# VectorE transposes the two 2-byte halves itself, with a lagging chain and moved issues, in a four-layer graph network on one core

## The chip, the cores and the metric

One core of a Trainium2 chip runs the kernel; the other cores are idle. The metric is the device time of one execution in microseconds. TensorE (PE) has a matrix queue and a weight-load queue (PEld), VectorE is DVE, ScalarE is ACT, GpSimd is POOL, and SyncE (SP) only issues transfers here. ACT issues transfers too.

## The reference

`x` is 2048 x 64, `adj` is 2048 x 2048 and holds zeros and ones. Four layers follow one another, each `x = layernorm(x + layer(x))`:

```python
# layer 0
deg = jnp.clip(jnp.sum(adj, axis=1, keepdims=True) + 1.0, 1.0, None)
h_neigh = (adj @ X + X) / deg
out = relu(concatenate([X, h_neigh], axis=1) @ W + b)
out / maximum(norm(out), 1e-12)
# layer 1
h = tanh(concatenate([X, tcol], axis=1) @ W1 + b1)
h @ W2 + b2 + adj @ (X @ B.T) - sum(adj, axis=1) * (X @ B.T)
# layer 2: the last up to 100 neighbours of a row, each weighted half as much as the next
rank = cumsum(adj != 0, axis=1); deg = rank[:, -1:]; k = minimum(deg, 100)
w = mask * where(rank - (deg - k) > 0, 0.5 ** (deg - rank), 0)
w @ (x @ weight) + bias
# layer 3
x_proj = tanh(|x|) * x / |x|
out = arctanh(|y|) * y / |y|, y = adj @ x_proj
out @ kernel + bias
```

## The kernel before

The nodes are cut into 16 blocks of 128 rows (NB), and the rows of `adj` into 4 chunks e of 512 (NE, CW). The transposed matrix stays in SBUF as `AT` (bf16), and the decayed weights of layer 2 as `WT` (int16, the exponent of a bf16).

**Loading.** Block m of `adj` (1 MB) goes to one of 8 slots (4 in `stage`, 4 in `WT`). Its lower half is two transfers issued by SP (`load_lower`), its upper half two issued by ACT (`load_upper`). Blocks 8 to 15 wait until the block in their slot is transposed. SP also issues the packed weights (417 KB), between blocks 0 and 1. In `pack(m)` (L247) POOL copies the upper two bytes of one set of words beside those of the other set, and `transposes(m)` (L464) moves the 1,024 pairs of a partition as 4-byte words through DVE's 32 x 32 transpose. `counts(e)` of PE waits for blocks 4e to 4e+3.

**Layer 0, the chain and a part of layer 1.** For each chunk e PE runs `counts(e)`, the 16 matmuls of `sums(0, e)` (`sum_block`, L687) with `degrees(e)` in their middle, `add_own`, and then `chain(n)` for n = 16e to 16e+15. A step of the chain is two matmuls of 512 columns (L752, L754) into one of two banks of `psC`; `take_chain(n)` of ACT (L361) evicts the bank, and step n+2 waits for it. `dense(0, e)` stands behind the second step. In chunk 3, 12 of the steps carry two matmuls each of layer 1.

ACT has, in order, 16 issues of blocks 0 to 7 ahead of its first eviction, and then in each chunk `take_counts`, `take_sum`, further issues (blocks 8 to 11 behind the sum of chunk 0, 12 and 13 behind that of chunk 1, 14 and 15 in the chain of chunk 1), and the 16 evictions.

DVE has in each chunk four `transposes`, `take_degrees`, `activate0` (which waits for POOL's `weigh` and for `dense(0, e)`), `combine0`, and `normalise` of the chunk before. `normalise` ends in `split`, which writes `XP`, the input of the next layer. POOL has the roots (`l2_root`, `var_root`, powers with a fixed time), `residual`, and `diagonals` (four instructions a chunk).

**Layers 1 to 3.** The rest of layer 1 (`transpose_x`, `hidden`, sums, `dense(1, e)`) stands behind the whole chain. Layers 2 and 3 have 64 sum matmuls each. PE runs groups 0, 1 and 2 (blocks 4g to 4g+3) over all four chunks, then the last group chunk by chunk with `dense(l, e)` behind it. Between the two layers DVE runs `add_residual`, `variance` and `exp_map(e)` for each chunk; `exp_map(e)` ends in `split`, and group g of layer 3 waits for `split` of chunk g. `take_sum(2, 3)` stands on ACT behind `norm_tanh(0)` and `squares(2, 2)`. Behind layer 3 come `norm_in`, `log_map` and `normalise(3, e)` on DVE, and 16 transfers of the output, issued by SP as the chunks of X come.

## Time and profile before

| | us |
|---|---|
| median of 3 runs | 185.96 (184.53 to 732.64) |
| profiled execution | 186.58 |
| its span | 184.6 |
| PE busy | 133.7 |
| DVE busy | 93.2 |
| ACT busy | 65.9 |
| POOL busy | 70.3 |

The span runs from the first to the last instruction; 1.98 us of the profiled execution lie around it. Rows of a timeline give the start, the duration, the engine, the line and the tiles, and in brackets the idle time before. Durations of neighbouring matmuls overlap, so their pitch is read from starts. `x8` is eight instructions merged into a row; a matmul with float32 operands runs as two.

### The profile page before, as it was taken

The page shows a single profiled execution, that of the slowest core. Times are in us where ns is not written, and L with a number is a line of the kernel's source. Part 1 is how long each engine was busy: PE and PEld are TensorE (multiplying, and loading weights), DVE is VectorE, ACT ScalarE, POOL GpSimd, SP SyncE. Part 2 cuts the span into 40 slices and gives each one's busy share as a digit, 9 for nine tenths or more (in the row PEclk, how much of TensorE's full clock was granted, in tenths as well). Part 3 has the DMA queues.
Part 4 walks back from the last instruction along what each step waited for, and adds up shares of the span by engine and source line. Part 5 has one row for each costly group of instructions (what it writes and reads, how often), then busy time and mean ns, then how long its engine had stood idle before and what let it go on. Part 6 is the DMA issues. An engine that isn't in the chain of part 4 may idle for free.

```text
span 184.6 us, 2088 instructions
## 1 busy us (share of the span) xinstructions
PE 133.7 (72%) x728; PEld 68.6 (37%) x728; DVE 93.2 (50%) x224; ACT 65.9 (36%) x122; POOL 70.3 (38%) x78
## 2 busy tenths in 40 slices
PE   0010799959998699889998999999992799970000
PEld 0000793511243135124543447874452544660000
DVE  0752773309948967951562000176326766068940
ACT  0001511138827664782767344400041300372100
POOL 0021535054596589374181000255308444032440
PEclk9999999978999999999999999999998599998555
DMA  6999999999999980000000000000000000000022
GB/s 140 264 260 326 340 340 325 209 208 276 269 286 221 249 172 12 0 0 0 4 0 0 0 0 4 0 0 0 4 0 0 0 0 2 0 0 0 0 56 57
DMA packets 13929, 18.58 MB, mean 101 GB/s; under 512 B 5472, under 2 KB 5600, under 8 KB 13920
## 3 DMA queue, kind: packets, MB, share of 16 engines
q1 hardware_dynamic: 8256, 9.81, 21.2%
q10 hardware_dynamic: 5664, 8.65, 18.1%
q8 instruction: 5, 0.08, 0.2%
q14 instruction: 4, 0.03, 0.1%
HBM read 17.93 MB, written 0.52 MB: 100 GB/s over the span
## 4 chain that ended last, share of the span: by engine, by line
PE 62%; ACTq 12%; ACT 9%; DVE 8%; issue 3%; POOL 2%; POOLq 1%; DVEq 0%
PE psS L687 20%; ACTq L328 12%; PE psC L687 10%; ACT WT L361 7%; PE psC L752 7%; PE psC L754 5%; PE psN L722 4%; PE psH L731 3%; PE psN L787 2%; PE psN L786 2%; PE psH L760 2%; POOL root L264 1%; PE psX L711 1%; PE psH L789 1%; PE psC L749 1%
## 5 line engine op out<-in xcount | busy, mean ns | idle before, releaser
L361 ACT ACTIVATE WT<-psC 128x512 int16<-128x512 f32 x64 | 36.2, 596 | 14.7 <-PE psC L754 9.4
L264 POOL TENSOR_TENSOR root<-var,power 128x4 f32<-128x4 f32 (+1 forms) x16 | 18.7, 1173 | 44.5 <-DVE var L516 27.5
L687 PE MATMUL psS<-AT,XP 128*128 128x512 bf16 x128 | 34.2, 403 | 0.0
L752 PE MATMUL psC<-AT,cb 128*128 128x512 bf16 x56 | 22.5, 403 | 6.7 <-ACT WT L361 6.0
L754 PE MATMUL psC<-AT,cb 128*128 128x512 bf16 x64 | 25.1, 393 | 0.0
L687 PEld LDWEIGHTS psS<-AT,XP 128*128 128x128 f16 x128 | 12.6, 104 | 17.1 <-issue 5.5
L247 POOL COPY stage<-stage 128x1024 bf16<-128x1024 bf16 x10 | 13.3, 1327 | 12.2 <-DMA stage<-adj 12.2
L711 PE MATMUL psX<-cb,XP 128*128 128x128 bf16 x32 | 4.0, 264 | 19.1 <-DVE XP L598 12.9
L464 DVE STREAM_TRANSPOSE AT<-stage 128x1024 f32<-128x1024 f32 x10 | 12.4, 1242 | 8.6 <-POOL stage L247 8.6
L687 PE MATMUL psC<-AT,XP 128*128 128x512 bf16 x64 | 15.4, 379 | 0.6 <-ACT WT L361 0.6
L752 PEld LDWEIGHTS psC<-AT,cb 128*128 128x128 bf16 x56 | 5.5, 99 | 26.4 <-ACT WT L361 24.8
L532 DVE TENSOR_TENSOR t<-psN,XB 128x256 f32<-128x256 f32 x6 | 2.5, 420 | 25.3 <-PE psN L787 19.7
L372 ACT ACTIVATE v<-t 128x256 f32<-128x256 f32 x12 | 5.0, 416 | 20.8 <-DVE t L532 16.0
L277 POOL TENSOR_TENSOR XB<-X,weights 128x256 f32<-128x256 f32 x12 | 9.2, 770 | 5.9 <-DVE X L521 5.9
L270 POOL TENSOR_SCALAR diag<-cb,ndeg 128x128 f16<-128x128 bf16 x16 | 11.0, 703 | 0.0
L464 DVE STREAM_TRANSPOSE AT<-WT 128x1024 f32<-128x1024 f32 x6 | 7.4, 1240 | 7.0 <-POOL WT L247 6.9
L521 DVE TENSOR_TENSOR X<-t,root 128x256 f32<-128x256 f32 x16 | 6.8, 423 | 8.3 <-POOL root L264 8.2
L711 PEld LDWEIGHTS psX<-cb,XP 128*128 128x128 f16 x32 | 3.0, 126 | 20.7 <-issue 14.0
L247 POOL COPY WT<-WT 128x1024 bf16<-128x1024 bf16 x6 | 8.0, 1346 | 5.0 <-DMA WT<-adj 5.0
L687 PEld LDWEIGHTS psC<-AT,XP 128*128 128x128 f16 x64 | 6.1, 99 | 7.2 <-issue 1.3
L355 ACT ACTIVATE stage<-psS 128x512 f32<-128x512 f32 x6 | 3.6, 597 | 13.9 <-PE psS L687 13.3
L283 POOL TENSOR_TENSOR nroot<-n,power 128x8 f32<-128x8 f32 x2 | 3.3, 1642 | 12.8 <-DVE n L552 12.8
(124 smaller groups left out, 214.2 us busy)
## 6 DMA issues: line engine op xcount, KB each, us to landing
stage<-adj ACTq DMA_DIRECT2D x20, 256.0 KB, 11.4
stage<-adj SPq DMA_DIRECT2D x20, 256.0 KB, 14.5
WT<-adj ACTq DMA_DIRECT2D x12, 256.0 KB, 16.2
WT<-adj SPq DMA_DIRECT2D x12, 256.0 KB, 17.9
out<-X SPq DMA_DIRECT2D x16, 32.0 KB, 1.6
weights<-weights_packed SPq DMA_DIRECT2D x1, 417.5 KB, 12.1
X<-x SPq DMA_DIRECT2D x2, 128.0 KB, 2.9
X<-x ACTq DMA_DIRECT2D x2, 128.0 KB, 3.6
```

The costliest lines, as they stand in the source:

```text
L247: nc.gpsimd.tensor_copy(halves[:, :, 1, :, 0], halves[:, :, 0, :, 1]).then_inc(packed, 1)
L264: nc.gpsimd.tensor_tensor(root[:, e, 0:n], var[:, e, 0:n], power[:, 0:n, 0:NR], ALU.pow).then_inc(root_ready, 1)
L270: last = nc.gpsimd.tensor_scalar(diag[:, c], C("paired"), ndeg[:, c:c + 1], None, ALU.mult)
L277: nc.gpsimd.tensor_tensor(XB[:, chunk(e)], X[:, chunk(e)], per_feature(W(f"b{l}")), ALU.add).then_inc(xb_ready, 1)
L328: act.dma_start(slot(slot_of(m))[QD * q:QD * (q + 1)], ad[m, q]).then_inc(filled[slot_of(m)], 16)
L361: nc.scalar.activation(WT[:, e, chain_block(bank, k)], psC[bank][:], ACT.Relu).then_inc(chain_taken, 1)
L464: nc.vector.transpose(words.rearrange("p c (k b) -> p k c b", k=2), src.rearrange("p k (c a) -> p k c a", a=QD)).then_inc(transposed, 1)
L687: ins = nc.tensor.matmul(bank, XP[:, l % 2, c], matrix, start=(c == 0), stop=last)
L711: ins = nc.tensor.matmul(psX[:, P * r:P * (r + 1)], XP[:, l % 2, NR * e + r], C("ident"), start=True, stop=True)
L722: ins = nc.tensor.matmul(psN[e % 2][:, D * r:D * (r + 1)], xt0[:, e % 2, P * r:P * (r + 1)], W("WA"), start=True, stop=True)
L752: nc.tensor.matmul(acc, C("past"), AT[:, c + 1, e], start=False, stop=False, skip_group_check=True)
L754: nc.tensor.matmul(acc, C("own"), AT[:, c, e], start=False, stop=True, skip_group_check=(k > 0)).then_inc(chain_ready, 1)
```

## The change

- `pack` is gone. `transposes(m)` waits for the transfers themselves and is two instructions. Each takes the upper two bytes of 1,024 words of a partition, read two bytes out of every four, and writes them two bytes out of every four.
- The weights go in two transfers: 128 columns (with `WA`, `b0`) behind block 0, the other 707 columns behind block 3. ACT issues blocks 4 to 7 one by one behind the four `take_xt(0, e)`, blocks 8 to 11 behind the first four evictions, 12 to 15 in the chain of chunk 1.
- The chain lags: steps 11 to 15, and 27 to 31, run inside the sums of the next chunk. Steps 42 to 55 follow the sums of chunk 3 with one matmul of layer 1 each in 12 of them. Ahead of chunk 3 PE runs parts of layer 1 (`transpose_x(1, 0)` and `(1, 1)`, `hidden(0)` and `(1)`, 12 sum matmuls), and steps 56 to 63 carry 12 sum matmuls of chunk 2 behind `dense(1, 0)`. The banks are dealt out anew for this.
- Layer 2 begins inside layer 1, and runs groups 2 and 3 together, chunk by chunk. ACT takes the sums 2 and 3 of layer 2 earlier. `exp_map` uses `t` times the root in place of X, and `normalise(2, e)` moves behind its `split`.
- In the tail ACT multiplies by the gain (`project`, 4 instructions of 128x64 a chunk) and rescales chunks 0 and 1 (`rescale`, 4 a chunk). `log_map` is cut in two. `diagonals` is one instruction a chunk.

```diff
-WCOLS = {"WA": 64, "WB": 64, "W1": 128, **{name: 64 for name in CENTRED}, "I": 64,
-         "b0": 64, "w1t": 1, "h_bias": 1, "t": 1}
+WCOLS = {"WA": 64, "b0": 64, "WB": 64, "W1": 128, **{name: 64 for name in CENTRED}, "I": 64,
+         "w1t": 1, "h_bias": 1, "t": 1}
...
         def sum_bank(l, e):
-            return psS[e % 2] if l == 0 else (psS + psC)[e]
+            return psS[0] if l == 0 else (psS[1], psN[1], psS[0], psC[0])[e]
...
-            return psN[e % 2] if l < 2 else (psN + [psX, psH])[e]
+            return psN[0] if l == 0 else (psN[0], psH)[e % 2] if l == 1 else (psN[0], psH, psX, psC[1])[e]
+
+        CHAIN_IN_SUMS = (0, 11, 27, 42)
+        CHAIN_LOOP = 56
+        CHAIN_ALL = NB * NE
...
             load_lower(0)
-            sp.dma_start(weights[:], wpack).then_inc(weights_loaded, 16)
-            for m in range(1, NB):
+            sp.dma_start(weights[:, 0:first], wpack[:, 0:first]).then_inc(own_weights_loaded, 16)
+            for m in range(1, NR):
+                load_lower(m)
+            sp.dma_start(weights[:, first:WTOT], wpack[:, first:WTOT]).then_inc(weights_loaded, 16)
+            for m in range(NR, NB):
                 load_lower(m)
...
-            def pack(m):
-                pool.wait_ge(filled[slot_of(m)], 16 * NQ * (fills_before(m) + 1))
-                halves = slot(slot_of(m)).rearrange("p Q j -> p (Q j)").bitcast(BF16).rearrange(
-                    "p (k h j w) -> p k h j w", k=2, h=2, w=2)
-                nc.gpsimd.tensor_copy(halves[:, :, 1, :, 0], halves[:, :, 0, :, 1]).then_inc(packed, 1)
...
+            def project(e):
+                act.wait_ge(gain_ready, e // 2 + 1)
+                rows = dense_bank(3, e)[:].rearrange("p (r f) -> p r f", r=NR)[:, :, 0:D]
+                for r in range(NR):
+                    c = NR * e + r
+                    ins = nc.scalar.activation(t[:, c], rows[:, r], ACT.Copy, scale=gain[:, c:c + 1])
+                ins.then_inc(projected, 1)
+
+            def rescale(e):
+                act.wait_ge(root_ready, layer_chunk(3, e) + 1)
+                for r in range(NR):
+                    c = NR * e + r
+                    ins = nc.scalar.activation(X[:, c], t[:, c], ACT.Copy, scale=root[:, e, 0, r:r + 1])
+                ins.then_inc(x_rescaled, 1)
...
-            for m in range(ALL_SLOTS):
+            for m in range(NR):
                 load_upper(m)
             for e in range(NE):
                 take_xt(0, e)
+                load_upper(NR + e)
             for e in range(NE):
                 take_counts(e)
+                if e >= 1 and e < 3:
+                    for n in range(CHAIN_IN_SUMS[e], NB * e):
+                        take_chain(n)
                 take_sum(0, e)
...
+                if e < 3:
+                    for n in range(NB * e, CHAIN_IN_SUMS[e + 1]):
+                        take_chain(n)
+                        if e == 0 and n < 4:
+                            load_upper(8 + n)
+                        if e == 1 and n < NB + 2:
+                            load_upper(n - NB + 12)
+                        if e == 1 and n >= NB + 4 and n < NB + 6:
+                            load_upper(n - NB + 10)
...
             take_sum(2, 1)
             squares(2, 0)
+            take_sum(2, 2)
             squares(2, 1)
-            take_sum(2, 2)
+            take_sum(2, 3)
             norm_tanh(0)
             squares(2, 2)
-            take_sum(2, 3)
...
             norm_squares(2)
             norm_squares(3)
+            project(0)
+            project(1)
+            take_logs(1)
             squares(3, 0)
             squares(3, 1)
-            take_logs(1)
+            project(2)
+            project(3)
+            rescale(0)
+            rescale(1)
             squares(3, 2)
             squares(3, 3)
...
-                dve.wait_ge(packed, m + 1)
-                src = slot(slot_of(m)).rearrange("p (k h) j -> p k h j", h=2)[:, :, 1]
-                words = AT[:, :, e, P * r:P * (r + 1)].bitcast(F32)
-                nc.vector.transpose(words.rearrange("p c (k b) -> p k c b", k=2),
-                                    src.rearrange("p k (c a) -> p k c a", a=QD)).then_inc(transposed, 1)
+                dve.wait_ge(filled[slot_of(m)], 16 * NQ * (fills_before(m) + 1))
+                halves = slot(slot_of(m)).rearrange("p Q j -> p (Q j)").bitcast(BF16).rearrange(
+                    "p (k h c a w) -> p k h c a w", k=2, h=2, a=QD, w=2)
+                to = AT[:, :, e, P * r:P * (r + 1)].rearrange("p c (k b h) -> p k c b h", k=2, h=2)
+                nc.vector.transpose(to[:, :, :, :, 0], halves[:, :, 0, :, :, 1])
+                nc.vector.transpose(to[:, :, :, :, 1], halves[:, :, 1, :, :, 1]).then_inc(transposed, 1)
...
+                step(nc.vector.tensor_tensor(gain[:, cs], gain[:, cs], root[:, e, 0], ALU.mult))
                 dve.wait_ge(tanh_ready, e + 1)
                 step(nc.vector.tensor_tensor(gain[:, cs], gain[:, cs], tanh[:, cs], ALU.mult))
-                step(nc.vector.tensor_tensor(u[:], X[:, cs], per_node(gain[:, cs]), ALU.mult))
+                step(nc.vector.tensor_tensor(u[:], t[:, cs], per_node(gain[:, cs]), ALU.mult))
                 split(3, e, u[:], PART_SCALE[3])
+                normalise(2, e)
...
-            for e in every:
+            for e in range(NE - 1):
                 pe.wait_ge(transposed, NR * (e + 1))
                 counts(e)
-                sums(0, e, range(0, 2))
-                degrees(e)
-                sums(0, e, range(2, 4))
+                for c in range(NB):
+                    sum_block(0, e, c)
+                    if c == NB // 2 - 1:
+                        degrees(e)
+                    n = CHAIN_IN_SUMS[e] + c // 2
+                    if c % 2 == 1 and n < NB * e:
+                        chain(n)
                 add_own(0, e)
-                for n in range(NB * e, NB * (e + 1)):
+                for n in range(NB * e, CHAIN_IN_SUMS[e + 1]):
                     chain(n)
                     if n % NB == 1:
                         dense(0, e)
...
             transpose_x(1, 0)
-            sums(1, 2, range(0, 1))
+            sums(1, 0, range(0, 1))
             hidden(0)
+            sums(1, 1, range(0, 1))
             transpose_x(1, 1)
-            sums(1, 2, range(1, 3))
+            sums(1, 0, range(1, 2))
             hidden(1)
...
+            for n in range(CHAIN_IN_SUMS[e], CHAIN_LOOP):
+                chain(n)
+                k = n - CHAIN_IN_SUMS[e] - 2
+                if k == -1:
+                    dense(0, e)
+                if 0 <= k < 8:
+                    sum_block(1, 1, NR + k)
+                if 8 <= k < 12:
+                    sum_block(1, 0, k)
...
+            sums(2, 0, range(2, 4))
+            sums(2, 1, range(2, 4))
+            dense(2, 0)
+            sums(2, 2, range(2, 4))
+            dense(2, 1)
+            sums(2, 3, range(2, 4))
+            dense(2, 2)
+            dense(2, 3)
```

## Rows read from the trace of the kernel before

**Rows 1.** The page's first part: busy time, share and instructions of each engine.

```profile
PE 133.7 (72%) x728; PEld 68.6 (37%) x728; DVE 93.2 (50%) x224; ACT 65.9 (36%) x122; POOL 70.3 (38%) x78
```

**Rows 2.** Timeline of PE: start, duration, line, tiles; the chunks' `counts`.

```profile
27.92 1.90 PE L731 MATMUL psH<-AT,cb 128*32 128x512 bf16 x16
...
49.36 1.05 PE L731 MATMUL psH<-AT,cb 128*32 128x512 bf16 x16
...
66.67 1.05 PE L731 MATMUL psH<-AT,cb 128*32 128x512 bf16 x16
...
82.45 1.05 PE L731 MATMUL psH<-AT,cb 128*32 128x512 bf16 x16
```

**Rows 3.** Chain that ended last, in order of time: start, duration, what.

```profile
57.49 0.61 ACT WT L361
58.15 0.39 PE psC L752
...
58.79 0.61 ACT WT L361
...
124.40 1.73 PE psC L687 x8
```

**Rows 4.** Timeline of PE from layer 2's first `dense` to layer 3's.

```profile
134.60 1.09 PE L789 MATMUL psN<-weights,stage 128*128 128x64 f32 x8
...
144.30 1.97 PE L789 MATMUL psH<-weights,stage 128*128 128x64 f32 x8 [4.28 <-ACT stage L355]
146.06 3.11 PE L687 MATMUL psS<-AT,XP 128*128 128x512 bf16 x8
...
159.37 1.15 PE L791 MATMUL psN<-weights,stage 128*128 128x128 f32 x8
```

**Rows 5.** Timeline of POOL: copies of blocks 0, 1, 2, the first `weigh`, copies 8, 11.

```profile
12.88 1.32 POOL L247 COPY stage<-stage 128x1024 bf16<-128x1024 bf16 x1 [3.02 <-DMA stage<-adj]
18.35 1.32 POOL L247 COPY stage<-stage 128x1024 bf16<-128x1024 bf16 x1 [4.15 <-DMA stage<-adj]
21.44 1.33 POOL L247 COPY stage<-stage 128x1024 bf16<-128x1024 bf16 x1 [1.77 <-DMA stage<-adj]
...
39.23 0.60 POOL L253 TENSOR_TENSOR Z<-Z,degp 128x256 f32<-128x256 f32 x1 [7.19 <-issue]
...
46.04 1.33 POOL L247 COPY stage<-stage 128x1024 bf16<-128x1024 bf16 x1 [0.76 <-DMA stage<-adj]
...
57.68 1.33 POOL L247 COPY stage<-stage 128x1024 bf16<-128x1024 bf16 x1 [0.79 <-DMA stage<-adj]
```

**Rows 6.** Groups by line: count, busy us, mean ns of one, idle before.

```profile
L361 ACT ACTIVATE WT<-psC 128x512 int16<-128x512 f32 x64 | 36.2, 596 | 14.7 <-PE psC L754 9.4 <-issue 3.1 <-DVE AT L464 1.2
...
L464 DVE STREAM_TRANSPOSE AT<-stage 128x1024 f32<-128x1024 f32 x10 | 12.4, 1242 | 8.6 <-POOL stage L247 8.6
...
L372 ACT ACTIVATE v<-t 128x256 f32<-128x256 f32 x12 | 5.0, 416 | 20.8 <-DVE t L532 16.0 <-DVE t L582 4.8
...
L377 ACT ACTIVATE tanh<-norm 128x4 f32<-128x4 f32 x4 | 0.8, 202 | 8.0 <-DVE norm L538 8.0
```

**Rows 7.** Timeline of DVE: block 3's transpose, degrees 0, first and last `split` of `exp_map`.

```profile
26.63 1.24 DVE L464 STREAM_TRANSPOSE AT<-stage 128x1024 f32<-128x1024 f32 x1
...
33.48 0.16 DVE L483 TENSOR_SCALAR ndeg<-psH 128x4 f32<-128x4 f32 x1
...
142.55 0.43 DVE L470 SCALAR_TENSOR_TENSOR XP<-u,XP 128x256 f16<-128x256 f32 x1
...
156.22 0.43 DVE L470 SCALAR_TENSOR_TENSOR XP<-u,XP 128x256 f16<-128x256 f32 x1
```

**Rows 8.** Busy time by stretch: PE, PEld, DVE, ACT, POOL, granted clock, DMA share, GB/s.

```profile
40.00:43.00 3.00, 3.00 (x9) 0.56 (x8) 1.83 (x3) 1.80 (x4) 2.35 (x2) 0.55 1.03 242
```

**Rows 9.** Timelines of ACT's and SP's queues: issues of blocks 8 to 11, of the output.

```profile
35.07 3.70 ACTq L328 DMA_DIRECT2D stage<-adj  x8
...
175.60 7.46 SPq L238 DMA_DIRECT2D out<-X  x16
```

250 lines of the change are left out of this document (139 added, 111 removed).

## The prediction

> **What bounds the kernel now.** I read the page's first part first: PE is busy in 72% of the span, every other engine in 50% or less [rows 1]. So PE is the spine, and the question is where it stands still. The timeline of PE gives the posts: the four chunks of layer 0 begin at 27.9, 49.4, 66.7 and 82.5 us [rows 2], layer 2's first `dense` is at 134.6 and layer 3's at 159.4 [rows 4]; the span ends at 184.6. The reader is to see that a chunk takes 21.4, 17.3 and 15.8 us. Eight sum matmuls take 1.73 us [rows 3], 0.216 each. So `counts` (1.0), 16 sums (3.45) and the small ones (0.35) make 4.8 us. A chain step is two such matmuls, 0.43; its eviction takes 0.60 [rows 6]. In the chain of waits two steps take 1.30 us (57.49 to 58.79) [rows 3]: a step alone costs 0.65 us, of which PE works 0.43, and a step with sums beside it costs PE only its 0.43. A chunk's 16 steps therefore leave some 3 us idle. Chunk 0 loses more: eight issues hold ACT for 3.70 us ahead of the first eviction [rows 9], and PE then ran at a granted clock of 0.55 [rows 8], near its lower level of 1.2 GHz. The other hole is between layers 2 and 3: PE waits 4.28 us for ACT's eviction of the last sum, then runs 8 sums in 3.11 instead of 1.89 us [rows 4].
>
> **The transposes.** The pair copy of 1.33 us [rows 5] goes from POOL, and DVE's one transpose of 1.24 us [rows 6, 7] becomes two. No row of before shows a transpose of 2-byte elements. Each of the two still has 1,024 elements in a partition. If time goes by elements each costs 1.24; if by bytes, half of it, 0.62. From above, an access of two bytes in four is shown only by POOL's copy, 1.33 for the same 1,024; against an unknown penalty of a strided half I keep twice the row, 2.48. I take 1.24, the row of the same operation with the same count: a pair is 2.4 us with the overlap, and 16 blocks add 19.8 us to DVE. The Trainium skill, "VectorE: DVE Perf Modes", section "What auto-detection actually checks", wants 16-bit elements at a step of one for two a cycle; here the step is two, so by it 0.62 is ruled out; no run here shows it yet.
>
> **Start.** In before, block 1 came 5.5 us behind block 0 and block 2 3.1 behind that (12.88, 18.35, 21.44) [rows 5]; the 2.4 us between are the 417 KB of weights. With 64 KB there, blocks 1 to 3 come 2.0 us earlier: block 3 at about 22.5. Its pair of transposes then ends at 25.0, where the one transpose ended at 27.9 [rows 7]. `own_part` ends by 24.1, since ACT no longer has 16 issues ahead of `take_xt`. PE begins chunk 0 at 25.0: **2.9 us gained**.
>
> **Chunk 0.** The first 7 us repeat (slow first sums included): own sum done at 32.0. Eleven steps follow, not 16. The eight issues now stand behind the first four evictions, so these cost about 1.0 each more; PE's last step ends at 41.2. But DVE is later: centring the weights (2.5 us) now stands ahead of block 4's transposes (27.8 to 30.2), degrees to 30.8, blocks 5 and 6 to 35.6. `activate0(0)` waits for POOL's first `weigh`, which in before began 5.7 us after its degrees (33.5, 39.23) with nothing shown to release it [rows 5, 7]; I keep that: 37.0. Then 2.7 us, and block 7 ends at 42.1. Chunk 1 begins at 42.1 against 49.4: **7.3 ahead**, with five steps left over.
>
> **Chunk 1.** PE: 4.8, five steps (2.15) inside, then two first steps, `dense`, nine more and four pairs of issues: done by about 57.2. DVE: `combine0(0)` to 44.4, block 8 to 46.8, `normalise(0, 0)` 48.0, degrees 48.6, block 9 51.0. Blocks 8 and 11 landed at 46.0 and 57.7 [rows 5], near 3.9 us apart; their upper halves are now issued two us earlier (33 for 35.1 [rows 9]). Block 10 at 51.8 gives 54.2, `activate0(1)` 56.9, block 11 59.3. DVE ends last: chunk 2 at 59.3 against 66.7, 7.4 ahead. So 32 pairs of halves do not cost PE 19.8 us; most lies under the chain, and 0.9 and 2.1 us of PE waiting are what they cost in chunks 0 and 1.
>
> **Chunk 2.** 59.3 plus 6.95, plus before's 11.0 from own sum to the end of the chain less six lagging steps (3.9), plus 5.0 for the layer 1 work put here: chunk 3 at 78.3 against 82.5. DVE: 61.6 after `combine0(1)`, four pairs, degrees, `normalise` and `activate0`: block 15 at 75.7, 2.6 us of slack.
>
> **Chunk 3 to layer 2.** Before: 52.2 us (82.45 to 134.6). Off: 5.0 of layer 1 done already, 1.7 (8 sums now behind `dense(2, 0)`), 0.6 of a wait between chain and layer 1. On: six more steps beside sums, 2.6. That is 47.5: layer 2's first `dense` at 125.8, **8.8 ahead**. The last `split` of layer 1 for chunk 3 ends near 93.1, when PE has arrived. Early parts of layer 2 hide the residual and root of `dense(1, 3)`.
>
> **Layer 2 to 3.** Before: 24.8 us. Both last sums are evicted before the tanhs, so `dense(2, 3)` ends near 133 and PE meets the first `split` at 133.6 instead of standing behind `dense(2, 3)` (144.3), although the split was done at 143.0 [rows 4, 7]. The four splits then come every 4.5 us (add 0.45, square 0.5, variance 0.6, map 2.5, `normalise` 0.45; the first and last of before are 13.7 apart [rows 7]): last at 145.7 to 147. PE's groups of 16 (3.46) leave 1.0 idle each. Layer 3's first `dense` at 147.8, 21.9 after layer 2's: **2.9 more, 11.7 ahead**.
>
> **Tail.** Before: 159.4 to 184.6, 25.2. SP's 16 issues take 7.46 us from the first chunk of X [rows 9], and 1.5 follow; later chunks are ready in time, so the end hangs on the first chunk, 16.2 after the post. `project` and `rescale` are 64 wide with a scale per partition; a small activation is 0.20, a 256-wide one 0.42 [rows 6], and neighbours overlap, so I put four at 1.0 us (bounds 0.5 and 1.7). The cut `log_map` gives 1.3, `project(2)` and `(3)` take 2.0 instead of DVE's 1.7 and the root waits with them: 0.5 gained, bounds 1.3 lost and 1.2 gained. The Trainium skill, "ScalarE: Activation LUTs", section "What ACT_TABLE_LOAD costs", gives 186 ns plus 0.833 a column plus 93 for the pointer, less 93 of overlap: by it, an estimate of 0.24 each, 0.96 for four.
>
> **The sum.** The span of 184.6 less 11.7 and 0.5 is 172.4. PE now stands still for 1 to 2 us near 41 and 57 while ACT issues; I add 1 us for a lower clock behind that (8 matmuls cost 1.2 more in rows 4). 173.4 and the 1.98 around the span: 175.4, say **175**. The profiled execution of before is 186.58, 0.6 above the median of 185.96, so against the median it is 0.94.
>
> **Rivals.**
> - *Halves are dear (slower).* At 2.48 each, every block holds DVE 2.4 us longer again. DVE has almost no gap from 16 to 76 us, so the last `counts` comes some 35 us later: 210. Each 0.1 us on a transpose costs 3.2 us less about 3 of slack once; the gain is gone from about 1.65 us a transpose. For it: no row of a 2-byte transpose. Against: DVE's ops with f16 output take the same 0.43 as float ones (the `split` in rows 7). 10%.
> - *The front gives little.* Blocks 9 to 15 land as late as before, or the clock stays low through the chains of chunks 0 and 1 (steps at 0.86): chunk 2 begins 3 us later, chunk 3 3 to 4: 178 to 182. For it: ACT's four issues in a row of evictions, and POOL's late first `weigh`. 17%.
> - *Halves are cheap.* At 0.62 the chain on PE and ACT sets chunks 1 and 2: 0.9 and 2.1 off: 172. 6%.
> - *Nothing to speak of.* ACT's order blocks elsewhere (the issue of block 15 waits for block 9's transposes, 51.0 against 54, in front of the evictions), and each stage gives back: 182 to 188. 7%.
>
> **Chances.** The forecast has 60%. The likeliest one's own range is 172 to 178. For 8 in 10 the range is 170.5 to 181.5: it leaves out the dear halves and the last rival. About 2% is what a measurement of this kernel can tell from no change; 182.2 and 189.7 are the bounds: faster 0.83, within 0.07, slower 0.10.
>
> **What would show it.** Two transposes a block at 1.24 us on DVE and none waiting for POOL; the first `counts` at 25, the others near 42, 59 and 78, with DVE ending the waits for the second and third; evictions of the sums of layer 2 with no wait of 4 us behind them; `dense` of layer 3 near 148; SP's 16 output issues unbroken. The prediction is wrong if a half costs over 1.5 us, if `activate0(0)` starts after 40, or if the clock is low past 50 us.

## The result and the profile after

| | before | after |
|---|---|---|
| median, us | 185.25 (183.28 to 732.64, 4 runs) | 174.26 (173.21 to 176.44, 4 runs) |
| ratio to before, 95% interval | | 0.942 [0.929, 0.955] |
| profiled execution, us | 186.58 | 174.74 |
| its span, us | 184.6 | 172.7 |

The time is 5.8% shorter. The forecast was 175.0 with a range of 170.5 to 181.5. The first part of the page of the changed kernel stands against [rows 1]:

```profile
PE 129.2 (75%) x728; PEld 67.6 (39%) x728; DVE 106.8 (62%) x238; ACT 71.5 (41%) x146; POOL 42.5 (25%) x50
```

DVE is 13.6 us busier than before, POOL 27.8 us less. The posts of the prediction are in PE's timeline (start, duration, engine, line and tiles; in brackets the idle time before and what ended it). They stand against [rows 2, 4]:

```profile
26.67 1.90 PE L779 MATMUL psH<-AT,cb 128*32 128x512 bf16 x16 [1.45 <-DVE AT L499]
43.69 1.05 PE L779 MATMUL psH<-AT,cb 128*32 128x512 bf16 x16 [0.48 <-DVE AT L499]
59.45 1.05 PE L779 MATMUL psH<-AT,cb 128*32 128x512 bf16 x16 [0.29 <-DVE AT L499]
78.83 1.05 PE L779 MATMUL psH<-AT,cb 128*32 128x512 bf16 x16
...
126.93 1.00 PE L845 MATMUL psN<-weights,stage 128*128 128x64 f32 x8
...
148.28 1.15 PE L847 MATMUL psN<-weights,stage 128*128 128x128 f32 x8
```

The starts of the four `counts`, of layer 2's first `dense` and of layer 3's cut the span into seven stretches:

| stretch, us | before | predicted | after |
|---|---|---|---|
| start to chunk 0 | 27.9 | 25.0 | 26.7 |
| chunk 0 | 21.4 | 17.1 | 17.0 |
| chunk 1 | 17.3 | 17.2 | 15.8 |
| chunk 2 | 15.8 | 19.0 | 19.4 |
| chunk 3 to layer 2's `dense` | 52.2 | 47.5 | 48.1 |
| layer 2's to layer 3's `dense` | 24.8 | 22.0 | 21.35 |
| tail | 25.2 | 24.7 | 24.4 |

Chunk 2 is longer by 3.6 us because work of layer 1 was moved into it. The other six are shorter: by 4.4 us in chunk 0, 4.1 behind chunk 3, 3.4 between layers 2 and 3, 1.55 in chunk 1, 1.25 at the start and 0.8 in the tail. Chunk 2 and the stretch behind chunk 3 together gain 0.45 us; no run below takes that part of the change back. The start of one and the same kernel moves by more than 1 us from run to run (24.9 to 26.7 us to the first `counts` in the runs that don't touch it), so the runs below are compared by the lengths of these stretches. Ratios leave out executions over 1.5% above the quickest of the same kernel, on both sides; in the early weights and the burst of issues the profiled execution is itself such a one. Ratios of nearly the same median also differ by 1% from one comparison to the next (174.26 us is 0.942 here, 174.04 us is 0.929 below), so differences of that size between them are not read.

The granted clock agrees. In a table of windows (window, its length, then busy time with count for PE, PEld, DVE, ACT and POOL, then the granted clock, the DMA share and GB/s) the place of [rows 8] now reads:

```profile
36.00:39.00 3.00, 1.92 (x8) 0.33 (x5) 2.86 (x4) 1.19 (x2) 0.00 (x0) 1.00 1.07 203
39.00:42.00 3.00, 1.78 (x7) 0.45 (x8) 2.83 (x7) 2.22 (x5) 1.06 (x1) 1.00 1.05 227
42.00:45.00 3.00, 2.32 (x22) 0.66 (x21) 2.90 (x6) 1.85 (x4) 0.00 (x0) 1.00 1.06 354
```

PE works 3.7 of the 6 us from 36 to 42, and its clock stays at the higher level of 2.4 GHz, where before it was at 0.55. DVE is busy in 8.6 of these 9 us.

### The profile page after: what moved, and what is told of

It reads as the page before. It is cut to its first block, busy times and chain, and to the rows that moved or that the text cites. A ratio compares the mean times of both kernels' runs of the same rounds, so it can differ in the third digit from the quotient of the medians.

```text
span 172.7 us, 2092 instructions
## 1 busy us (share of the span) xinstructions
PE 129.2 (75%) x728; PEld 67.6 (39%) x728; DVE 106.8 (62%) x238; ACT 71.5 (41%) x146; POOL 42.5 (25%) x50
## 4 chain that ended last, share of the span: by engine, by line
PE 41%; DVE 28%; DMA 13%; ACT 6%; issue 5%; POOL 4%; POOLq 1%; ACTq 0%; DVEq 0%
PE psS L733 13%; DMA WT<-adj 11%; DVE AT L499 4%; PE psN L733 4%; DVE AT L498 4%; PE psC L733 3%; PE psC L800 3%; PE psC L802 3%; DMA X<-x 3%; PE psX L809 2%; POOL nroot L288 2%; ACT WT L363 1%; PE psX L759 1%; POOL root L269 1%; PE psH L779 1%
## 5 line engine op out<-in xcount | busy, mean ns | idle before, releaser
L269 POOL TENSOR_TENSOR root<-var,power 128x4 f32<-128x4 f32 (+1 forms) x16 | 18.7, 1170 | 44.6 <-DVE var L550 21.3
L800 PE MATMUL psC<-AT,cb 128*128 128x512 bf16 x56 | 21.4, 383 | 4.4 <-ACT WT L363 4.4
L802 PE MATMUL psC<-AT,cb 128*128 128x512 bf16 x64 | 24.2, 379 | 0.0
L733 PEld LDWEIGHTS psS<-AT,XP 128*128 128x128 f16 x128 | 11.9, 100 | 18.7 <-DVE XP L504 3.9
L498 DVE STREAM_TRANSPOSE AT<-stage 128x1024 bf16<-128x1024 bf16 x10 | 13.1, 1314 | 1.9 <-DMA stage<-adj 1.8
L499 DVE STREAM_TRANSPOSE AT<-stage 128x1024 bf16<-128x1024 bf16 x10 | 12.7, 1268 | 0.0
L282 POOL TENSOR_TENSOR XB<-X,weights 128x256 f32<-128x256 f32 x12 | 9.3, 771 | 11.9 <-DVE X L555 11.9
L498 DVE STREAM_TRANSPOSE AT<-WT 128x1024 bf16<-128x1024 bf16 x6 | 7.9, 1324 | 4.0 <-DMA WT<-adj 3.9
L258 POOL TENSOR_TENSOR Z<-Z,degp 128x256 f32<-128x256 f32 x4 | 2.5, 614 | 29.4 <-DVE ndeg L517 29.4
L263 POOL TENSOR_TENSOR ssroot<-ss,power 128x4 f32<-128x4 f32 x4 | 4.1, 1030 | 22.1 <-DVE ss L528 22.1
L550 DVE TENSOR_REDUCE var<-v 128x4 f32<-128x260 f32 x8 | 3.2, 417 | 10.1 <-ACT v L374 10.1
L733 PE MATMUL psN<-AT,XP 128*128 128x512 bf16 x32 | 9.2, 379 | 0.0
L770 PE MATMUL psN<-weights,diag 128*128 128x64 f32 x32 | 7.7, 422 | 2.0 <-DVE Z L510 1.9
L566 DVE TENSOR_TENSOR t<-psN,XB 128x256 f32<-128x256 f32 x3 | 1.3, 425 | 11.9 <-PE psN L843 7.4
```

Of the source, the lines that this page charges most:

```text
L269: nc.gpsimd.tensor_tensor(root[:, e, 0:n], var[:, e, 0:n], power[:, 0:n, 0:NR], ALU.pow).then_inc(root_ready, 1)
L282: nc.gpsimd.tensor_tensor(XB[:, chunk(e)], X[:, chunk(e)], per_feature(W(f"b{l}")), ALU.add).then_inc(xb_ready, 1)
L498: nc.vector.transpose(to[:, :, :, :, 0], halves[:, :, 0, :, :, 1])
L499: nc.vector.transpose(to[:, :, :, :, 1], halves[:, :, 1, :, :, 1]).then_inc(transposed, 1)
L733: ins = nc.tensor.matmul(bank, XP[:, l % 2, c], matrix, start=(c == 0), stop=last)
L770: ins = nc.tensor.matmul(psN[e % 2][:, D * r:D * (r + 1)], xt0[:, e % 2, P * r:P * (r + 1)], W("WA"), start=True, stop=True)
```

## The experiments

Twelve kernels ran, each beside the kernel before on the same chip. Ratios are to that kernel; posts are from each run's own trace. What a diff does not show is as in the kernel it starts from.

**The pairing put back.** The changed kernel, but with `pack` on GpSimd and DVE's one 4-byte transpose, in the order of the kernel before:

```diff
+            for m in range(NR + 1):
+                pack(m)
             for e in range(NE - 1):
+                pack(NR * e + 5)
                 weigh(e)
+                pack(NR * e + 6)
...
-                nc.vector.transpose(to[:, :, :, :, 0], halves[:, :, 0, :, :, 1])
-                nc.vector.transpose(to[:, :, :, :, 1], halves[:, :, 1, :, :, 1]).then_inc(transposed, 1)
+                nc.vector.transpose(words.rearrange("p c (k b) -> p k c b", k=2),
+                                    src.rearrange("p k (c a) -> p k c a", a=QD)).then_inc(transposed, 1)
```

> The changed kernel with GpSimd's pairing copy put back and one 4-byte transpose a block; all else stays. Theory A (the rearrangement makes the gain, the dearer transposes lie under the chain of PE and ACT): DVE loses about 20 us of busy time, yet the span stays near that of the changed kernel's 172.7, 172 to 176; the first weigh comes late again (its first instruction has to be waited for some 7 us behind the copies), so chunk 1 begins near 45 instead of 43.7. Rival B (taking the pairing away is itself a good part of the gain, since every block waited for POOL and POOL's copies held DVE's instructions): 178 or more. Rival C (the doubled transposes cost PE time in the changed kernel): under 171.

Measured: 179.11 us, ratio 0.958 [0.951, 0.964]. Chunk 0 is 21.0 us again (17.0 in the changed kernel) and chunk 1 17.5 (15.8); the rest keeps its length (19.4, 48.1, 21.3). POOL's timeline shows why, and PE's shows the price:

```profile
30.72 1.33 POOL L259 COPY WT<-WT 128x1024 bf16<-128x1024 bf16 x1 [1.66 <-DMA WT<-adj]
39.39 0.60 POOL L265 TENSOR_TENSOR Z<-Z,degp 128x256 f32<-128x256 f32 x1 [7.34 <-issue]
39.95 2.56 POOL L259 COPY WT<-WT 128x1024 bf16<-128x1024 bf16 x2
```

```profile
46.41 1.90 PE L792 MATMUL psH<-AT,cb 128*32 128x512 bf16 x16 [5.65 <-DVE AT L511]
```

The first `weigh` (L265) follows a copy that ended at 32.05, waits 7.34 us for nothing that the profile shows, and holds the copies of blocks 6 and 7 behind it. PE then stands for 5.65 us, and its granted clock is 0.50, the lower level, from 45 to 48: the same 16 matmuls take 1.90 us here and 1.05 in the changed kernel. So the rearrangement is worth some 7 us with the pairing kept (179.11 against 186.53 for the kernel before in the same comparison), and taking the pairing away 4.4 (spans of 177.1 and 172.7) to 4.9 us (medians) more.

**The halves alone.** The kernel before with only `pack` gone and the two 2-byte transposes in its place:

```diff
-            for m in range(NR + 1):
-                pack(m)
...
+                nc.vector.transpose(to[:, :, :, :, 0], halves[:, :, 0, :, :, 1])
+                nc.vector.transpose(to[:, :, :, :, 1], halves[:, :, 1, :, :, 1]).then_inc(transposed, 1)
```

> The kernel before with the two 2-byte transposes in place of pairing and one transpose, and nothing else. Theory A: DVE gains 20 us of work, but the four chunks begin within 1 us of 27.9, 49.4, 66.7 and 82.5, because the chain on ACT and PE ends later than block 7's and block 11's transposes: time 183 to 186, the same as before. Rival B (the pairing was a cost on the path): 181 or less. Rival C (DVE becomes the bound of the chunks): 190 or more.

Measured: 187.21 us (10 runs), ratio 1.021 [1.015, 1.027], against a before of 186.53 over all its runs in this comparison: between no change and 2% slower. Yet the late `weigh` is gone here too:

```profile
33.96 0.61 POOL L246 TENSOR_TENSOR Z<-Z,degp 128x256 f32<-128x256 f32 x1 [23.49 <-DVE ndeg L470]
```

It starts at once when the degrees are there, and chunk 0 still takes 21.4 us, as before. ACT's timeline shows what holds it now (ACTq is ACT's own issuing of transfers), and the windows show the clock:

```profile
35.23 0.69 ACT L341 ACTIVATE sum<-psS,xs 128x512 f32<-128x512 f32 x1 [3.96 <-PE psS L688]
35.24 3.70 ACTq L314 DMA_DIRECT2D stage<-adj  x8
38.99 1.08 ACT L347 ACTIVATE WT<-psC 128x512 int16<-128x512 f32 x2 [3.07 <-DVE AT L452]
```

```profile
36.00:39.00 3.00, 1.43 (x10) 1.05 (x8) 2.97 (x5) 0.01 (x1) 0.00 (x0) 0.97 1.06 199
39.00:42.00 3.00, 2.36 (x6) 0.52 (x6) 2.83 (x7) 2.10 (x4) 1.06 (x1) 0.50 1.07 199
42.00:45.00 3.00, 3.00 (x8) 0.52 (x8) 2.90 (x6) 1.96 (x4) 0.00 (x0) 0.50 1.06 272
```

Eight issues in a row keep ACT from the first eviction of the chain, PE stands, and 6 us at half the clock follow. Chunk 0 thus had two hindrances, POOL's late `weigh` and ACT's burst of issues. They did not weigh the same: one lay under the other. The first of these rows is from the kernel before, the second from the halves alone; each is the last transpose of block 7:

```profile
44.96 1.25 DVE L464 STREAM_TRANSPOSE AT<-WT 128x1024 f32<-128x1024 f32 x1
```

```profile
42.34 1.27 DVE L452 STREAM_TRANSPOSE AT<-WT 128x1024 bf16<-128x1024 bf16 x1
```

In the kernel before, block 7 was transposed by 46.2, and `counts` of chunk 1 came at 49.36 [rows 2]: even with the late `weigh`, DVE was done 3.15 us before PE. With the halves alone it is done by 43.6, and `counts` comes at 50.1. So the chain behind the burst ended last, and taking away the late `weigh` alone could bring nothing. In the run above the burst is gone, and the late `weigh`, which comes at 39.4 as before, ends last. Chunk 0 is 21.0 and 21.4 us with one of the two gone and 17.0 with both gone.

Of these 4.4 us the lag of five steps takes 1.4: without it (the run without lag, below) chunk 0 is 18.4. The other 3.0 lie between that run and the halves alone. Both have the halves and all 16 steps in chunk 0, and in both the transposes are done before PE is. What differs ahead of that point is the burst, the issues of blocks 4 to 7, the place of the weights and some order on DVE and GpSimd; with the issues of blocks 4 to 7 put back (below) chunk 0 is no longer than in the changed kernel. So the 3.0 us are left to the burst, by elimination and not by a run of its own. The kernel before with nothing but its burst taken apart, or nothing but the late `weigh` cured and the copies kept, was not run.

Measured apart the two parts give 4.2% and at best nothing; together they give 5.8%.

**The burst of issues put back.** If that reading is right, the changed kernel with the old burst must lose in chunk 0:

```diff
+                if e == 0:
+                    for m in range(8, 12):
+                        load_upper(m)
+                if e == 1:
+                    load_upper(12)
+                    load_upper(13)
                 if e < 3:
                     for n in range(NB * e, CHAIN_IN_SUMS[e + 1]):
                         take_chain(n)
-                        if e == 0 and n < 4:
-                            load_upper(8 + n)
-                        if e == 1 and n < NB + 2:
-                            load_upper(n - NB + 12)
```

> The changed kernel, with ACT's issues of the upper halves of blocks 8 to 11 in a row behind the sum of chunk 0 and of 12 and 13 behind the sum of chunk 1, as in the kernel before, and not one behind each of the first evictions. Theory A (the part of the rearrangement that makes the halves affordable is this one): ACT issues for 3.7 us, PE finishes the sums and stands for 3 us or more, the first eviction comes 3.5 to 4.3 us after the sum, eleven steps at 0.65 then end near 45, chunk 1 begins 1.5 to 3 us later against the first counts than in the changed kernel (18.5 to 20 after it, 17.0 there), with a granted clock under 0.8 somewhere in chunk 0 or 1, and the time is 176 to 179. Rival B: DVE's transposes and the blocks' landing set chunk 1 in any case, the burst lies beside them: chunk 1 comes 17 to 17.6 after chunk 0 and the time is 174 to 175.2.

Measured: 176.12 us (174.03 to 177.68, 4 runs). ACT's timeline and the windows of the profiled execution, which was 177.68:

```profile
33.41 0.69 ACT L357 ACTIVATE sum<-psS,xs 128x512 f32<-128x512 f32 x1 [4.60 <-PE psS L749]
33.42 5.05 ACTq L330 DMA_DIRECT2D stage<-adj  x8
38.52 1.08 ACT L363 ACTIVATE WT<-psC 128x512 int16<-128x512 f32 x2 [4.42 <-issue]
```

```profile
36.00:39.00 3.00, 0.00 (x0) 0.00 (x0) 2.86 (x7) 0.48 (x1) 0.00 (x0) 0.77 1.07 199
39.00:42.00 3.00, 2.83 (x7) 0.65 (x8) 2.93 (x5) 1.83 (x5) 1.06 (x1) 0.50 1.05 260
42.00:45.00 3.00, 2.99 (x8) 0.39 (x6) 2.86 (x7) 2.22 (x4) 0.64 (x1) 0.59 1.06 358
```

Chunk 0 takes 19.95 us there (26.27 to 46.22), 2.9 more than in the changed kernel, with PE idle from 36 to 39 and then at the lower clock: what theory A says, in the stage where it says it. But this is one of the two longer executions. The four took 177.7, 177.2, 175.0 and 174.0 us; the quicker two lie where rival B puts them, and their ratio, 0.936 [0.925, 0.947], is that of the changed kernel. None of the quicker ones was profiled, so whether the burst costs them 2 to 3 us too, beneath a start that itself moves by up to 1.8 us, stays open. The burst's part in chunk 0 thus rests on the 3.0 us above; this run agrees in one trace and does not settle it in the time.

**The pairing put back, with GpSimd's first multiplication moved.** The first run's 7.34 us belong either to the first `tensor_tensor` as such or to its place behind the copies. One small multiplication ahead of the first copy tells them apart:

```diff
+            nc.gpsimd.tensor_tensor(warm[:], power[:, 0, 0:NR], power[:, 1, 0:NR], ALU.mult)
             pool.wait_ge(consts_loaded, 16)
             for m in range(NR + 1):
                 pack(m)
```

> As the run with GpSimd's pairing put back into the changed kernel, plus one small multiplication on GpSimd (128 x 4, its result is not used) right behind its fixed-time powers and ahead of the first pair copy. In the run without it GpSimd's first weigh, its first tensor_tensor, stood 7.34 us after the copy ahead of it with nothing that released it, and held the copies of blocks 6 and 7, so chunk 1 began 21.0 us after chunk 0 (17.0 in the changed kernel). Theory A: these 7 us are the start of the first tensor_tensor as such, wherever it comes; put ahead of the loading they cost nothing. Then the first weigh follows its releaser within 0.5 us, chunk 1 begins 16 to 17.5 us after chunk 0, and the time is 172 to 175, level with the changed kernel or 1 us below, since DVE has 20 us less to do. Theory B: the 7 us belong to the place (a semaphore seen late, or copies that are still running): the weigh still waits some 7 us, chunk 1 begins 20 us or more after chunk 0, and the time stays at 178 to 180.

Measured: 173.89 us (172.26 to 174.16), ratio 0.931 [0.922, 0.939]. POOL's timeline:

```profile
9.21 0.38 POOL L304 PARTITION_ALL_REDUCE xs<-xs  x1 [8.29 <-issue]
16.86 0.19 POOL L305 TENSOR_TENSOR warm<-power 128x4 f32<-128x4 f32 x1 [7.28 <-issue]
17.01 3.79 POOL L260 COPY stage<-stage 128x1024 bf16<-128x1024 bf16 x3
...
32.86 0.61 POOL L266 TENSOR_TENSOR Z<-Z,degp 128x256 f32<-128x256 f32 x1 [0.24 <-DVE ndeg L532]
```

The 7.3 us have moved with the first `tensor_tensor`, and `weigh` follows its releaser in 0.24 us. At the front they delay block 0's transpose to 18.4 us (12.9 in the changed kernel), which DVE makes up by chunk 0 (27.05 for 26.67). Chunk 0 takes 15.3 us and chunk 1 16.4, all at the full granted clock. Theory A holds. The Trainium skill, "GPSIMD Engine Reference", section "2.1 Instruction dispatch", says that the first call to freshly loaded code pays a load of about 6 us with no visible instruction; the trace agrees in kind, and its figures are higher: 7.3 here and 8.0 in the mixed run below. That these waits are such a load is the page's reading; the rows show only that they come once and go with the first `tensor_tensor`. So what the halves brought in the changed kernel was not that VectorE transposes them, but that the 7 us of waiting left the path: with the pairing kept and this one instruction added, the kernel is level with the changed one (medians of 173.89 and 174.26; ratios 0.931 and 0.942, the intervals overlap), and DVE is 94.0 us busy instead of 106.8.

**A third half.** The changed kernel with the first of the two transposes done twice (`step` waits for the instruction's end):

```diff
+                step(nc.vector.transpose(to[:, :, :, :, 0], halves[:, :, 0, :, :, 1]))
                 nc.vector.transpose(to[:, :, :, :, 0], halves[:, :, 0, :, :, 1])
```

> The changed kernel with the first of the two transposes of every block done twice (same data, with a wait between), so each block costs DVE about 1.3 us more, 21 us in all; it measures what a dearer transpose would have cost. Theory A (DVE has only some 5.6 us of waits for data and 2 us of slack ahead of the last counts): 13 to 16 us longer than the changed kernel, 187 to 190. Rival (much of DVE's work hides under the chain, as the first 20 us of the change did): 6 us longer or less, 180.

Measured: 186.85 us (10 runs), 12.6 above the changed kernel; the span is 13.4 longer. PE's `counts`:

```profile
29.44 1.90 PE L780 MATMUL psH<-AT,cb 128*32 128x512 bf16 x16 [2.03 <-DVE AT L500]
49.05 1.05 PE L780 MATMUL psH<-AT,cb 128*32 128x512 bf16 x16 [2.93 <-DVE AT L500]
70.04 1.90 PE L780 MATMUL psH<-AT,cb 128*32 128x512 bf16 x16 [5.53 <-DVE AT L500]
91.77 1.05 PE L780 MATMUL psH<-AT,cb 128*32 128x512 bf16 x16
```

The added half, with the wait behind it, puts off the next one by 1.34 us on average (1.31 to 1.36). Sixteen of them are 21.4 us of DVE, and 12.6 to 13.4 arrive at the end: the changed kernel has 8 to 9 us of slack on DVE up to the last block. The ratio is 1.013 [1.007, 1.020], and over all executions the medians are 186.85 and 186.53: 21.4 us more on DVE use up the whole gain.

**No lag in chunks 0 and 1.** The chain's steps 11 to 15 and 27 to 31 go back ahead of the next chunk:

```diff
-        CHAIN_IN_SUMS = (0, 11, 27, 42)
+        CHAIN_IN_SUMS = (0, 16, 32, 42)
```

> The changed kernel with chunks 0 and 1 running all their 16 chain steps alone behind their own sums (no step lags into the next chunk's sums); the later part stays. Theory A (a step beside sums saves 0.22 us, and PE's last step and block 7's and 11's transposes end within 0.5 us of each other in the changed kernel, so the chain sets chunks 1 and 2 without the lag): chunk 1 begins near 46.5, chunk 2 near 63, chunk 3 near 80.3; 1.5 to 2 us longer, 175.5 to 176.5. Rival (DVE alone sets the chunks): chunk starts unchanged, 174.3.

Measured: 174.04 us, ratio 0.929 [0.923, 0.935]. Chunks 0 to 2 take 18.4, 16.3 and 17.2 us, 51.9 together against 52.2 with the lag, and from chunk 1 on no `counts` waits for DVE. The lag takes 1.4 us out of chunk 0 and 0.5 out of chunk 1, and chunk 2 gives 2.2 back: in these chunks it is worth nothing (0.2 us, less than the runs differ by).

**The issues of blocks 4 to 7 first**, as before, ahead of `take_xt`:

```diff
-            for m in range(NR):
+            for m in range(ALL_SLOTS):
                 load_upper(m)
             for e in range(NE):
                 take_xt(0, e)
-                load_upper(NR + e)
```

> The changed kernel with ACT's issues of blocks 4 to 7 ahead of its first eviction again, as in the kernel before; the later issues stay. In the changed kernel block 3 landed at 24.1, 0.4 us earlier than before and not 2.0, and blocks 1, 2 and 3 came 3.8 us apart instead of 3.1. Theory A (ACT's queue runs dry from 7 to 14 us, and SP's alone moves less): blocks 2 and 3 come 3.1 us apart again and earlier, but the first eviction waits for the issues (17 us), so the first counts are at 27 to 28; time within 1 us of the changed kernel. Rival (the spacing has another cause, such as the split weights): spacing stays 3.8 and the start is later by the issues, 1 us or more slower.

Measured: 174.95 us, ratio 0.938 [0.933, 0.942]. The first `counts` is at 27.0 and chunk 0 takes 15.4, chunk 1 17.7 and chunk 2 19.4 us. DVE no longer waits for block 6 (1.29 us in the changed kernel), but for block 8, and PE waits 2.27 us for DVE at the end of chunk 1: the three together are 52.5 us against 52.2. The `counts` of chunk 1 come at 42.4, against 42.0 to 43.7 in the traces that leave the front of the changed kernel alone: what the start loses, chunk 0 gives back.

**The weights early**, as before, ahead of block 1:

```diff
-            for m in range(1, NR):
-                load_lower(m)
             sp.dma_start(weights[:, first:WTOT], wpack[:, first:WTOT]).then_inc(weights_loaded, 16)
-            for m in range(NR, NB):
+            for m in range(1, NB):
                 load_lower(m)
```

> The changed kernel with the second part of the weights issued right behind the first one, between blocks 0 and 1. Theory A (the weights take 2.0 us of the queue wherever they stand): block 3 lands 2 us later, first counts at 28.5, and since block 4 lands where it did, chunk 1 is within 1 us of 43.7: time within 1 us of the changed kernel. Rival (the move of the weights is what starts the kernel earlier): 2 us longer, 176.

Measured: 177.53 us (174.86 to 180.81), ratio 0.942 [0.936, 0.948] over the two quicker ones. The profiled execution is one of 179.04, so its stretches are not used. The ratio shows no loss; the two quicker executions took 174.86 and 176.02 us, so a loss of about 1 us can't be told from none.

**Layer 2's sums late on ACT**, in the order of the kernel before:

```diff
-            take_sum(2, 2)
             squares(2, 1)
-            take_sum(2, 3)
+            take_sum(2, 2)
             norm_tanh(0)
             squares(2, 2)
+            take_sum(2, 3)
```

> The changed kernel with ACT's order between layers 2 and 3 as before: the evictions of sums 2 and 3 of layer 2 behind squares and the first tanh. Theory A (the 4.28 us wait of the kernel before came from this order): the wait for the last sum's eviction comes back, PE begins layer 3 3 to 4 us later than 134.6, at 137.5 to 139, and with the lower clock level behind it the end is 2 to 4 us later: 176.5 to 178.5. Rival (DVE's splits set layer 3 anyway, every 4.3 us): group 0 is late but the last group is not, under 1 us longer, 175.

Measured: 177.89 us, ratio 0.954 [0.949, 0.959]. PE's timeline, against [rows 4]:

```profile
136.24 1.10 PE L845 MATMUL psC<-weights,stage 128*128 128x64 f32 x8 [3.16 <-ACT stage L357]
137.18 1.49 PE L733 MATMUL psS<-AT,XP 128*128 128x512 bf16 x4
138.46 1.91 PE L733 MATMUL psN<-AT,XP 128*128 128x512 bf16 x4
```

The hole of 3.16 us is back, and four matmuls behind it take up to 1.91 us, where they take 1.03 in the changed kernel. From layer 2's `dense` to layer 3's it is 24.1 us against 21.35: 2.7 us. The medians are 3.6 us apart (177.89 and 174.26), more than this stretch; in the profiled execution 0.95 us of the rest is in chunk 1, which the edit does not touch (see the clock, below).

**The same order alone in the kernel before:**

```diff
             squares(2, 0)
-            squares(2, 1)
             take_sum(2, 2)
+            squares(2, 1)
+            take_sum(2, 3)
             norm_tanh(0)
             squares(2, 2)
-            take_sum(2, 3)
```

> The kernel before with nothing but ACT's two evictions of layer 2's sums 2 and 3 moved ahead, as in the changed kernel. Theory A: PE begins layer 3's sums at the first split, near 143 instead of 146; the last group stays bound by the last split (156.6), so 0 to 1.5 us are gained: 183.5 to 185.5. Rival: the whole 2.9 us of this stretch are gained by it, 182.

Measured: 184.96 us (10 runs), ratio 0.999 [0.993, 1.004]; the stretch is 23.8 us against 24.8. The wait moves from ACT's sum to DVE's `split` (2.98 us). So the order gives 1.0 by itself and 2.7 in the changed kernel, and the rest of the change gives 0.7 without it (24.8 to 24.1): the two need each other. That the rest is the shortened `exp_map` with its later `normalise` is the likely reading; no run has that part alone.

**The old tail.** DVE applies the gain and normalises, ACT has no `project` and no `rescale`:

```diff
-            project(0)
-            project(1)
-            take_logs(1)
...
-            rescale(0)
-            rescale(1)
+            take_logs(1)
...
-            log_map(1)
+            log_in(1)
+            log_map(1)
+            normalise(3, 0)
+            normalise(3, 1)
```

> The changed kernel with the tail of the kernel before: DVE applies the gain, adds and normalises chunk by chunk behind one log_map a pair, and ACT has no project and no rescale. Theory A (the prediction): the tail is then 0.5 us longer, with bounds of 1.3 shorter and 1.2 longer: in the trace of the changed kernel layer 3's first dense is 24.4 us ahead of the end, in the kernel before 25.2, so this run shows some 25.0 and a time of 174.0 to 175.5. Rival B: the project and rescale steps of ACT carry more of the gain than the prediction gave them, and the tail is over 1.5 us longer (over 175.7). Up to layer 3's first dense the posts are those of the changed kernel under both.

Measured: 174.75 us, ratio 0.939 [0.930, 0.949]. From layer 3's first `dense` (146.54) to the end (171.8) it is 25.3 us against 24.4. The new tail is worth 0.8 us against this trace; as it is 24.4 to 25.0 in the other traces with it, 0.3 to 0.8, too little for the times to show.

**A mixture.** GpSimd pairs blocks 5, 7, 9 and 11 only, the small multiplication stands ahead, and the chain lags three steps more in chunks 0 and 1 and two more in chunk 2:

```diff
-        CHAIN_IN_SUMS = (0, 11, 27, 42)
+        CHAIN_IN_SUMS = (0, 8, 24, 40)
+        MIXED = (5, 7, 9, 11)
...
+                if m in MIXED:
+                    dve.wait_ge(packed, MIXED.index(m) + 1)
```

> A try at a better version: GpSimd pairs blocks 5, 7, 9 and 11 only (one 4-byte transpose each), DVE moves the halves of the other twelve, the small multiplication of the run above stands ahead, and the chain lags by three steps more in chunk 0, three in chunk 1 and two in chunk 2. DVE has 5 us less to do in chunks 0 and 1. If DVE were still what sets these chunks, as the prediction had it (0.9 and 2.1 us of PE waiting), the time is 171.5 to 173. If the chain on PE and ACT and the landing of the blocks set them, as the waits of 0.48 and 0.29 us in the changed kernel and the run without the lag say, it stays at 173.5 to 175.

Measured: 174.85 us, ratio 0.940 [0.930, 0.949]: no gain. With eight steps in chunk 0 PE is done sooner, at 38.3, and stands until block 7 is transposed:

```profile
41.99 1.05 PE L800 MATMUL psH<-AT,cb 128*32 128x512 bf16 x16 [3.70 <-DVE AT L512]
```

A granted clock of 0.67 from 42 to 45 follows. The longer lag gathers PE's short waits between chain steps into one.

## Why the prediction was right, and where its steps were not

**The halves.** The term was 1.24 us each. DVE's groups by shape (count, busy us, mean ns of one, idle time before them):

```profile
L498 DVE STREAM_TRANSPOSE AT<-stage 128x1024 bf16<-128x1024 bf16 x10 | 13.1, 1314 | 1.9 <-DMA stage<-adj 1.8
L499 DVE STREAM_TRANSPOSE AT<-stage 128x1024 bf16<-128x1024 bf16 x10 | 12.7, 1268 | 0.0
```

1.31 and 1.27 us, and 1.22 from start to start, as for the 4-byte one (1.24): at this stride time goes by elements and not by bytes, and the dear half and the cheap half are both out. The rule of the Trainium skill that the prediction weighed ("VectorE: DVE Perf Modes", section "What auto-detection actually checks") had ruled out 0.62; the trace agrees. The price that I put on a dearer half, 3.2 us for each 0.1 us, was too high: the third half adds as much as 0.67 us on each of the 32, which by that price is 18.4 us after the slack of 3, and it cost 12.6 to 13.4. The slack was mis-sized, 8 to 9 us and not 3. The break-even lies just under 1.22 + 0.67 = 1.89 us from start to start, an estimate, where I had 1.65.

**Start: 1.25 us gained, 2.9 predicted.** The step "blocks 1 to 3 come 2.0 us earlier" went wrong. It moved before's rows and kept block 3 only 9.6 us behind block 0. In this trace the first and the fourth block were 11.2 us apart on DVE, with waits for the transfers:

```profile
12.91 1.31 DVE L498 STREAM_TRANSPOSE AT<-stage 128x1024 bf16<-128x1024 bf16 x1
16.50 1.33 DVE L498 STREAM_TRANSPOSE AT<-stage 128x1024 bf16<-128x1024 bf16 x1
20.37 1.32 DVE L498 STREAM_TRANSPOSE AT<-stage 128x1024 bf16<-128x1024 bf16 x1 [1.09 <-DMA stage<-adj]
24.14 1.31 DVE L498 STREAM_TRANSPOSE AT<-stage 128x1024 bf16<-128x1024 bf16 x1 [0.67 <-DMA stage<-adj]
```

ACT now issues blocks 4 to 7 among its evictions of `take_xt`, and blocks 2 and 3 are waited for all the same. The size of the miss is partly chance. In the four other traces that leave this front alone (no lag, late sums, old tail, burst) the first and the fourth block are 10.2 to 10.8 us apart and the first `counts` is at 25.5, 25.5, 24.9 and 26.3: the spacing is longer than predicted in all, the post of 25.0 is within their spread. With the weights back in front, or the issues, no loss could be measured: no gain of either move shows in the time.

**Chunk 0: right by two errors.** I kept the 5.7 us that POOL's first `weigh` had waited [rows 5]. It does not wait now:

```profile
32.37 0.61 POOL L258 TENSOR_TENSOR Z<-Z,degp 128x256 f32<-128x256 f32 x1 [22.32 <-DVE ndeg L517]
```

But block 6 landed only at 36.1, where I had its halves done by 35.6, so `activate0(0)` began at 38.5 and not at 37.0, and block 7 was transposed at 43.6, not at 42.1. So chunk 0 began and ended 1.6 us late (chunk 1 at 43.7 for a predicted 42.1), and its length is the predicted one only because the wait that I kept for POOL put off `activate0(0)` by 1.4 us (37.0 for 35.6), about as much as the wait for block 6 (1.29), which I did not see. That is luck. That the `weigh` of before had no releaser should have been a question of its own: on it hangs what leaving out the pairing brings, and the prediction gave that 20 us of cost on DVE and no gain. It was also the place to ask why the wait of before cost nothing there (block 7 done 3.15 us before PE), and what it would cost once PE came earlier.

**Chunks 1 and 2.** DVE ends both waits, as predicted, but they are 0.48 and 0.29 us for 0.9 and 2.1: PE itself was done 2 us later than I had it in each chunk. For chunk 0 this holds of this execution more than of the kernel: ACT's fourth pair of issues took 2.13 us in it, and PE was done 16.5 us after the first `counts`. In the late sums and the old tail, with the same front, that pair took 0.9 us, PE was done after 14.7 and 15.4 us, and then waited 2.56 and 1.70 us for DVE. Chunk 1 is 1.4 us shorter than predicted because DVE makes up the 1.6 us by which it began late. I had block 9 done at 51.0 and block 10 waited for until 51.8; block 9 was done at 51.83, and block 10 followed without a wait:

```profile
51.85 1.33 DVE L498 STREAM_TRANSPOSE AT<-stage 128x1024 bf16<-128x1024 bf16 x1
...
58.13 1.26 DVE L499 STREAM_TRANSPOSE AT<-stage 128x1024 bf16<-128x1024 bf16 x1
```

Block 11's second half ends at 59.39, where the prediction had 59.3, and chunk 2 begins at 59.45. It is 0.4 us longer than predicted.

**Clock.** The 1 us added for a lower clock near 41 and 57 was not needed in the profiled execution. The pairing put back, the halves alone, the mixture and the profiled execution of the burst all show such a clock, each behind one stand of PE (2.21 to 5.65 us). In the changed kernel ACT's issues lie between evictions, and PE's longest stand in chunk 0 is 1.60 us. But its front does not always escape. The late sums run the same front, and there `counts` of chunk 1 found the lower clock:

```profile
42.70 1.90 PE L779 MATMUL psH<-AT,cb 128*32 128x512 bf16 x16 [2.56 <-DVE AT L499]
```

Chunk 1 took 16.7 us for 15.8 behind it. The term of 1 us was thus right for one execution of this front and not for another.

**Chunk 3 to layer 2** came 0.6 longer than predicted; which of its terms was short stays open. **Layer 2 to 3** was predicted 22.0 and took 21.35. PE waits for `split` at each group and nowhere for a sum:

```profile
134.55 1.04 PE L733 MATMUL psS<-AT,XP 128*128 128x512 bf16 x4 [0.54 <-DVE XP L504]
...
138.82 1.04 PE L733 MATMUL psS<-AT,XP 128*128 128x512 bf16 x4 [0.64 <-DVE XP L504]
...
143.09 1.04 PE L733 MATMUL psS<-AT,XP 128*128 128x512 bf16 x4 [0.64 <-DVE XP L504]
```

The groups come every 4.27 us, for 4.5 predicted. The run with late sums shows the mechanism and its size.

**Tail.** Four acts of `project` were priced at 1.0 us:

```profile
156.07 0.93 ACT L391 ACTIVATE t<-psN,gain 128x64 f32<-128x64 f32 x4 [0.80 <-DVE gain L613]
...
163.70 7.46 SPq L249 DMA_DIRECT2D out<-X  x16
```

They take 0.93, SP's issues are unbroken at 7.46, and the tail is 0.8 shorter for 0.5 predicted.

**The sum.** The seven stretches and the clock were predicted to take 11.2 us off the span and took 11.9. The terms for the start (1.6 too good), chunks 2 and 3 (0.4 and 0.6 too good), and on the other side chunk 1 (1.4), the clock (1.0), layer 2 (0.6) and the tail (0.3) were off: errors of up to 1.6 us that cancel. That the sum came within 0.7 us is in part luck. What the prediction missed is behind the sum: of the two hindrances in chunk 0 it reckoned with the issues alone, and left the late `weigh` in.

## What to carry to other kernels

Where one hindrance lies under another, taking away the lower one looks worth nothing (here 0 to 2% lost), and taking away the upper one brings the lower one to the end of the stage; read from the trace which ends last and by how much, and test them together before dropping either. Read every idle time with no shown releaser as a question of its own: here one 128 x 4 multiplication, put where its wait could be made up, brought as much as taking all 16 pair copies off GpSimd. Transfers issued by a computing engine are better put between its instructions than in a row ahead of one that TensorE waits for (3.0 us of chunk 0 here, with the reservation above).
